# One reciprocal for two steps, a later normalisation, and a new order of SP's transfers in a three-layer attention kernel with a nearest-neighbour branch

## What is computed

```
def chunk_attn(q = k = v = ctx):    # 8 heads of 16 channels, chunks of 64 tokens
    project ctx with W_in to queries, keys and values
    scores = q_chunk . k_chunk / 4 + mask
    attn   = softmax(scores)        # over the 64 keys of the chunk
    return (attn . v_chunk) W_out + b_out
x = layernorm(chunk_attn(ctx) + x)     # layer 0
x = layernorm(chunk_attn(ctx) + x)     # layer 1
idx = top_k(-distance(ctx[0:3] of all token pairs), 30)     # layer 2, the neighbours
feat = spherical coordinates of ctx[0:3][idx] - ctx[0:3]
att = softmax(three small batch-normalised layers of feat)
x = x + sum over the 30 neighbours of att * x[idx]
x = layernorm(chunk_attn(ctx) + x)     # layer 3
```

## Time and profile before

| | us |
|---|---|
| median of 3 executions | 6674.75 (6666.72 to 6677.72) |
| profiled execution | 6667.89 |
| span of the core in it | 6665.9 |
| busy: PE | 5685.7 (85%) |
| busy: DVE | 5886.1 (88%) |
| busy: ACT | 4461.5 (67%) |
| busy: POOL | 3249.3 (49%) |
| mean granted TensorE clock | 0.904 |

### The profile page before, as it was taken

How to read it: one execution, slowest core, us unless ns; L and a number is a source line. 1 busy time by engine, 2 the same in 40 slices (tenths; PEclk the granted TensorE clock), 3 DMA queues, 4 the chain that set the end, 5 groups by cost and what they waited for, 6 DMA issues and landing times. The chain is left out here.

```text
span 6665.9 us, 228315 instructions
## 1 busy us (share of the span) xinstructions
PE 5685.7 (85%) x83284; PEld 3456.0 (52%) x83284; DVE 5886.1 (88%) x8332; ACT 4461.5 (67%) x17049; POOL 3249.3 (49%) x3279
## 2 busy tenths in 40 slices
PE   7888888888888888888888888888839949999998
PEld 3454545455555545545554555555423337677776
DVE  7999999999999999999999999999946588777776
ACT  7787878787787878787877878788822533333333
POOL 3455655555555555555655555555550023333332
PEclk9999988898888999898898998998859979999999
DMA  2333333233333333333233333333241013333332
GB/s 48 89 97 85 93 91 91 84 91 87 100 92 91 97 85 94 91 90 91 85 92 102 91 91 92 93 91 90 80 118 35 0 38 90 90 83 89 87 84 78
DMA packets 633780, 564.50 MB, mean 85 GB/s; under 512 B 535517, under 2 KB 557277, under 8 KB 598653
## 3 DMA queue, kind: packets, MB, share of 16 engines
q1 hardware_dynamic: 632572, 548.75, 29.1%
HBM read 380.55 MB, written 67.24 MB: 67 GB/s over the span
## 5 line engine op out<-in xcount | busy, mean ns | idle before, releaser
L703 ACT ACTIVATE prob<-SC,row_max 128x64 f32<-128x64 f32 x6144 | 1835.3, 327 | 671.7 <-DVE row_max L1032 664.8
L817 POOL TENSOR_TENSOR prob<-prob,row_rec 128x512 f32<-128x512 f32 x768 | 829.9, 1081 | 1897.7 <-DVE row_rec L1040 1897.1
L703 ACT ACTIVATION_READ_ACCUMULATOR prob<-SC,row_max 128x1 f32 x6144 | 1349.0, 220 | 0.0
L1024 DVE FIND_INDEX8 nbr<-top,dist 128x8 uint16<-128x1024 f32 x1024 | 1235.8, 1220 | 0.0
L1017 DVE MAX8 top<-dist 128x8 f32<-128x1024 f32 x1024 | 1194.1, 1207 | 12.6 <-DVE y_b L1055 10.3
L610 PE MATMUL PT<-ident,prob 128*128 128x128 f32 x3072 | 516.1, 295 | 573.9 <-ACT prob_t L710 563.2
L610 PEld LDWEIGHTS PT<-ident,prob 128*128 128x128 f32 x3072 | 383.6, 151 | 1076.8 <-issue 1033.2
L589 PE MATMUL SC<-k_bd,q_t 128*64 128x256 f32 x6144 | 935.8, 430 | 0.0
L1019 DVE MATCH_REPLACE8 dist<-top,dist 128x1024 f32<-128x1024 f32 x768 | 925.2, 1210 | 0.0
L1816 DVE TENSOR_TENSOR d_oh_a<-lo,iota_a 128x4096 bf16<-128x4096 bf16 x256 | 584.4, 2293 | 255.2 <-PE DM L1667 254.8
L1708 ACT ACTIVATE dense<-DM 128x512 f32<-128x512 f32 x512 | 305.6, 597 | 746.3 <-PE DM L1667 746.1
(11 more groups left out here) (194 smaller groups left out, 9538.6 us busy)
## 6 DMA issues: line engine op xcount, KB each, us to landing
low_all<-low_scratch SPq DMA_DIRECT2D x256, 1024.0 KB, 4.9
k_bd<-k_t SPq DMA_DIRECT2D x3072, 16.0 KB, 1.9
placed<-compact SPq DMA_DIRECT2D x256, 192.0 KB, 3.7
ctx<-in_ctx SPq DMA_DIRECT2D x32, 512.0 KB, 4.0
mask<-in_mask SPq DMA_DIRECT2D x32, 512.0 KB, 7.8
xb<-in_x SPq DMA_DIRECT2D x32, 512.0 KB, 4.3
x_scratch<-xb SPq DMA_DIRECT2D x32, 512.0 KB, 4.7
y_scratch<-y_b SPq DMA_DIRECT2D x32, 512.0 KB, 6.6
```

The lines of the kernel that those rows point to most:

```text
L703: last = act.activation(prob[:, s % 4, g * CHUNK:(g + 1) * CHUNK], SC[:, s % 2, g * CHUNK:(g + 1) * CHUNK], ACT.Exp, bias=row_max[:, s % 2 ...
L817: pool.tensor_tensor(pr, pr, row_rec[:, r % 2, :].unsqueeze(2).to_broadcast([128, 8, CHUNK]), ALU.mult).then_inc(normed, 1)
L1024: last = dve.max_index(nbr[:, uu % BPB, t, k * 8:(k + 1) * 8], best, row)
```

## The change

Four edits. The lag of the normalisation goes from one step to two (`LAG_SUM`), and `row_sum` and `row_rec` get four buffers in place of two. DVE takes one reciprocal of 16 columns in every even step, for the two steps before it, in place of one of 8 columns in each step. POOL normalises step s-2 in its step s. On SP, the three pieces on the low index bytes (out, tiles 0 and 1, the later tiles) go to the head of the step, before the keys; and the indices themselves (`nbr`) go out in step 7, after the keys, and not in step 5.

```diff
--- before.py
+++ after.py
@@ -37,7 +37,7 @@
 HALF = T // 2
 
 
-LAG_SUM, LAG_T, LAG_PV, LAG_O, LAG_Y = 1, 3, 4, 5, 6
+LAG_SUM, LAG_T, LAG_PV, LAG_O, LAG_Y = 2, 3, 4, 5, 6
 LAG_BN, LAG_LN, LAG_TOP = 7, 8, 2
 
 
@@ -192,8 +192,8 @@
         prob = sb("prob", [128, 4, 512])
         prob_t = sb("prob_t", [128, 2, 512])
         row_max = sb("row_max", [128, 2, 8])
-        row_sum = sb("row_sum", [128, 2, 8])
-        row_rec = sb("row_rec", [128, 2, 8])
+        row_sum = sb("row_sum", [128, 4, 8])
+        row_rec = sb("row_rec", [128, 4, 8])
         o_t = sb("o_t", [128, 2, HALF])
         y_b = sb("y_b", [128, 2, T])
         stats = sb("stats", [128, 2, 6])
@@ -427,8 +427,31 @@
                 return real(i, v + BPB, BPB)
 
             def step(i, s):
+                v = lagging(i, s, LOW_OUT_AT)
+                if v is not None:
+                    b = i * BPB + v
+                    sp.wait_ge(low_ready, START + b + 1)
+                    alone(sp)
+                    rows = dram["low"][b].rearrange("t (g q k) -> q g t k", q=4, k=KP)
+                    for q in range(4):
+                        sp.dma_start(rows[q], low[32 * q:32 * q + 32, :, :]).then_inc(low_out, 16)
+                v = lagging(i, s, LOW_IN_AT)
+                if v is not None:
+                    sp.wait_ge(low_out, START + (i * BPB + v + 1) * 64)
+                    alone(sp)
+                    for t in range(2):
+                        load_low(i, v, t)
+                at = lagging_tile(i, s, SELECT_AT)
+                if at is not None and at[1] + 2 < NT:
+                    load_low(i, at[0], at[1] + 2)
                 if real(i, s, STEPS) and s % 2 == 0 and real(i, s // 2 + KEY_BUFS - 1, STEPS // 2):
                     keys_of_heads(i, s // 2 + KEY_BUFS - 1)
+                v = lagging(i, s, LOW_IN_AT + 1)
+                if v is not None:
+                    b = i * BPB + v
+                    sp.wait_ge(topped, START + (b + 1) * NT)
+                    alone(sp)
+                    sp.dma_start(dram["nbr"][b], nbr[:, v % BPB, :, :].rearrange("p t k -> p (t k)")).then_inc(nbr_out, 16)
                 ub = s // BSTEPS + 1
                 if real(i, s, STEPS) and real(i, ub, BPB):
                     if s % BSTEPS == COLS_OUT_AT:
@@ -450,23 +473,6 @@
                     landed(sp, x2_out, i, v)
                     alone(sp)
                     sp.dma_start(xb[:, v % BPB, :], dram["x"][i * BPB + v + BPB]).then_inc(x_in[v % BPB], 16)
-                v = lagging(i, s, LOW_OUT_AT)
-                if v is not None:
-                    b = i * BPB + v
-                    sp.wait_ge(topped, START + (b + 1) * NT)
-                    alone(sp)
-                    sp.dma_start(dram["nbr"][b], nbr[:, v % BPB, :, :].rearrange("p t k -> p (t k)")).then_inc(nbr_out, 16)
-                    sp.wait_ge(low_ready, START + b + 1)
-                    alone(sp)
-                    rows = dram["low"][b].rearrange("t (g q k) -> q g t k", q=4, k=KP)
-                    for q in range(4):
-                        sp.dma_start(rows[q], low[32 * q:32 * q + 32, :, :]).then_inc(low_out, 16)
-                v = lagging(i, s, LOW_IN_AT)
-                if v is not None:
-                    sp.wait_ge(low_out, START + (i * BPB + v + 1) * 64)
-                    alone(sp)
-                    for t in range(2):
-                        load_low(i, v, t)
                 v = lagging(i, s, 6)
                 if v is not None:
                     b = i * BPB + v
@@ -475,9 +481,6 @@
                     sp.dma_start(dram["y3"][b], y_b[:, y_half(LAYERS * v + 2), :]).then_inc(y3_out, 16)
                     if more(i, v):
                         sp.dma_start(mask[:, v % BPB, :], dram["mask"][b + BPB].broadcast_to([128, T])).then_inc(mask_in[v % BPB], 16)
-                at = lagging_tile(i, s, SELECT_AT)
-                if at is not None and at[1] + 2 < NT:
-                    load_low(i, at[0], at[1] + 2)
                 v = lagging(i, s, OWN_AT)
                 if v is not None:
                     b = i * BPB + v
@@ -698,10 +701,10 @@
                 if real(i, s, STEPS):
                     act.wait_ge(maxed, START + i * STEPS + s + 1)
                     act.wait_ge(transposed, at_least(i, START + i * STEPS + s - 3, START))
-                    act.wait_ge(recip_ready, at_least(i, START + i * STEPS + s - 1, START))
+                    act.wait_ge(recip_ready, at_least(i, START + i * (STEPS // 2) + s // 2 - 1, START))
                     for g in range(8):
                         last = act.activation(prob[:, s % 4, g * CHUNK:(g + 1) * CHUNK], SC[:, s % 2, g * CHUNK:(g + 1) * CHUNK], ACT.Exp,
-                                              bias=row_max[:, s % 2, g:g + 1], accum_out=row_sum[:, s % 2, g:g + 1])
+                                              bias=row_max[:, s % 2, g:g + 1], accum_out=row_sum[:, s % 4, g:g + 1])
                     last.then_inc(exped, 1)
                 r = s - LAG_T
                 if real(i, r, STEPS):
@@ -812,9 +815,9 @@
                 u = s // BSTEPS
                 r = s - LAG_SUM
                 if real(i, r, STEPS):
-                    pool.wait_ge(recip_ready, START + i * STEPS + r + 1)
+                    pool.wait_ge(recip_ready, START + i * (STEPS // 2) + r // 2 + 1)
                     pr = prob[:, r % 4, :].rearrange("p (h k) -> p h k", h=8)
-                    pool.tensor_tensor(pr, pr, row_rec[:, r % 2, :].unsqueeze(2).to_broadcast([128, 8, CHUNK]), ALU.mult).then_inc(normed, 1)
+                    pool.tensor_tensor(pr, pr, row_rec[:, r % 4, :].unsqueeze(2).to_broadcast([128, 8, CHUNK]), ALU.mult).then_inc(normed, 1)
                 part = s % BSTEPS - SPLIT_AT
                 if real(i, s, STEPS) and 0 <= part <= SPLITS and real(i, u + 1, BPB):
                     split_row(i, u + 1, part, START + i * STEPS + r + 1)
@@ -1034,10 +1037,10 @@
                 if real(i, s, STEPS) and s % BSTEPS == MASK_AT and real(i, u + 1, BPB):
                     mask_rows(i, u + 1)
                 r = s - LAG_SUM
-                if real(i, r, STEPS):
-                    dve.wait_ge(exped, START + i * STEPS + r + 1)
-                    dve.wait_ge(normed, at_least(i, START + i * STEPS + r - 1, START))
-                    dve.reciprocal(row_rec[:, r % 2, :], row_sum[:, r % 2, :]).then_inc(recip_ready, 1)
+                if real(i, r, STEPS) and r % 2 == 0:
+                    dve.wait_ge(exped, START + i * STEPS + r + 2)
+                    dve.wait_ge(normed, at_least(i, START + i * STEPS + r - 2, START))
+                    dve.reciprocal(row_rec[:, r % 4:r % 4 + 2, :], row_sum[:, r % 4:r % 4 + 2, :]).then_inc(recip_ready, 1)
                 r = s - LAG_Y
                 if real(i, r, STEPS) and r % 4 == 3:
                     jj, uu = place(r)
```

## The result

The changed kernel takes 6757.17 us (median of 4 executions, 6746.05 to 6760.6) against 6675.35 us before (4 executions, 6666.72 to 6677.72): a ratio of 1.0122, with an interval of 1.0109 to 1.0136. It is slower, as forecast, but by 82 us and not by 25, and outside my range (6600 to 6750).

What follows compares the result with a forecast made beforehand. The prediction took DVE to be the bound. Its terms, -109.8 (low bytes) + 62 (keys) + 84 (clock) - 11 (reciprocals), gave +25 us: 6693 on the profiled execution, 6700 on the median's scale, range 6600 to 6750.

Steps and rivals of the forecast that it cites:

- What the change takes away: Step 2: tile 6 is issued where the keys were, so DVE's wait for low bytes goes; -109.8 us.
- What the new order adds, the keys: Step 6's keys queue behind tile 1's load; PE idles in step 10, DVE waits in steps 10 and 11; +62 us.
- two patterns: DVE's wait in steps 10 and 11 alternates by batch between 2.8 and 1.3 us; mean 2.05, over 30 batches.
- the late pattern: The batch worked out first: tile 1 goes out behind the late last fetch, and DVE waits 2.8 us in steps 10 and 11.
- The clock: PE's clock falls to 0.50 behind the new idle stretch in step 10; 2.8 us in each of 30 batches, +84 us.
- Rival (1): Scores of step 10: PE's clock does not fall at the new gap, or its loss is absorbed; -59, 6616; chance 0.20.
- Reciprocals: DVE issues 384 fewer, the 384 left are wider; -11 us, bounds -23 and +19.
- The estimate of -41 us: Net for the reciprocals by the skill's fixed cost of a DVE operation, 384 fewer giving 60 us; not adopted.
- Normalisation later: POOL's product a step later is hidden behind other work, and nothing is won; 0 us in the sum.
- Rival (4): Step 13: the late normalisation is exposed too, 2 us in each of 30 batches; +85, 6760; chance 0.10.

Runs made afterwards that it cites:

- filler_16: The changed kernel with 16 products of 128x128 f32 put into PE's step 10, ahead of its wait for the keys; 6699.8 us, ratio 1.0041.
- late_loads_first: The kernel before with only the loads of tiles 2 to 7 moved ahead of the keys of their step; 6560.56 us, ratio 0.983.
- late_norm_only: The changed kernel with SP's order as before; the paired reciprocals and the later normalisation stay; 6604.82 us, ratio 0.9902.
- sp_order_only: The kernel before with all of the new order on SP; reciprocals and normalisation lag as before; 6710.36 us, ratio 1.0066.
- keys_split: The changed kernel with four of step 6's eight keys issued ahead of the loads of tiles 0 and 1, four behind; 6698.03 us, ratio 1.0033.

## Why the prediction was wrong, by its own steps

**What the change takes away: right.** -109.8 us, and the table of after has no such wait.

**What the new order adds, the keys: right in mechanism, 62 us forecast, 78 us measured** (`filler_16`, where the clock is at 1.00). I had two patterns, 2.8 and 1.3 us, and took their mean, with the sentence that the batches "go to and fro" between them. That sentence failed. In batches 4 to 31 of the kernel before, the last fetch ended late (over 13.6 us after the maxima of step 6) in 13 of 28; after, in 26 of 28. The mean went from 13.4 to 14.3 us. It is not the new gap that does this: late_loads_first has neither stall nor gap, and there it is 27 of 28 (mean 14.3). I read it so, without a run that tests this alone: with the stall of step 2 gone, DVE comes to step 6 sooner while PE's fetch doesn't, and the late pattern holds nearly always. 2.8 us in each of 30 batches is 84 us. A pattern that a stall made was carried into a kernel without the stall. PE's idle stretch I had put at 4.7 us; it is 4.4. In part the sum was off: 5.7 us for eight keys puts the start of the last at 2022.8, not 2023.0.

**The clock: right, 84 forecast, 75 measured.** That is 2.5 us a batch against my 2.8. Rival (1) falls with it. The loss is 75 of 6757 us, 1.1%. The Trainium skill (TensorE: Matmul & The Clock Gate, Part 1) puts the ramp at under 1% of a typical kernel's span, but it says so of the warm-up of a kernel's first matmuls. Here the clock fell in 30 batches, so the sentence was no support for rival (1). The loss is small as a share, but nearly as large as the whole net effect of the change.

**Scores elsewhere: not forecast.** 171.3 less 153.5 leaves 17.8 us of new waits outside steps 10 and 11, 12 of them in steps 0 and 1. They come with the late normalisation: late_norm_only has 17.1 us of them, sp_order_only 0.7. By what path is open.

**Reciprocals: right.** The source view of after has them:

```profile
L1043 DVE RECIPROCAL row_rec<-row_sum x384: 229/240/254, 43.8 to 4924.7; 128x16 f32<-128x16 f32 x192
```

240 ns, as forecast. With DVE's waits and the longer `hot` taken out, odd steps became 0.07 us shorter and even ones 0.04 longer, over 384 of each: -11 us, the forecast figure. The price by start-to-start time held. The estimate of -41 us, from the Trainium skill (VectorE: DVE Perf Modes, the part on the TRN2 errata), did not.

**Normalisation later: this step failed, on both sides.** I had written "so nothing is won", since DVE did not wait for exponentials. I had looked at who waits for the normalised values and not at what POOL does in the time that it no longer waits. There is a gain: the coordinates leave 3.2 us sooner, which by itself takes 75 us of low-byte wait away (late_norm_only, 0.9902). In the full change this cannot be seen, for SP's new order removes the same wait already; two cures of one stall don't add up. And there is a loss, which I had not listed in any form: POOL, moved in time, runs into `hot`, 30 us. Beside the new order the pairing leaves only costs and the small gain of the reciprocals: 30 (`hot`) + 23 (scores, 215.0 less 191.6) - 11 = +42 us. The attention stretch is 40.8 us longer than in sp_order_only (4887.3 less 4846.5), and so the full change is worse than its order alone: 6757 against 6710.

**Rival (4)** gave 6760, within 3 us of the result, and is still false. Its mechanism was PE waiting for late products, and the place was right: PE waits 33 times for 81.5 us, against 9.9 before, and 30 of these, 79.3 us, are for the product of POOL's step 13, one in each batch. But DVE has no wait for scores in steps 12 to 16 in this kernel, and late_norm_only has the same wait on PE (91.2 us) and is faster than before. It lies beside other work, as the forecast had it.

**Range and sum.** The upper end, 6751 (+76), was the late pattern in every batch with the full clock loss. Keys and clock together stayed 44 us below that (153 against 197). What carried the time over it are the two costs that come with the late normalisation and stood in no term: the `hot` collision and the scores elsewhere, 48 us. From +25: +16 (keys) -9 (clock) +18 (other scores) +30 (`hot`) = +80.

## What to carry to other kernels

Before transfers are moved up in an in-order queue, list for each step what stands behind each of its waits afterwards; one load that waits, ahead of eight small copies in one step of 24, turned a gain of 1.2% into a loss of 1.2%, and moving only the loads of tiles 2 to 7 gained 1.7%. When a change takes a recurring stall away, don't average over the patterns that the stall made: ask which of them is left. And an engine off the critical path that gets free earlier has two effects to price, what it releases sooner and what it now runs beside.

## What the runs showed of the hardware

**DVE and POOL hold each other up.** The bf16 table of line 1094 takes 1.27 us alone and 2.05 us in the mean of step 2 when a POOL `tensor_tensor` is under way. In the rows above, POOL's product ran to 2015.34 and DVE's had come at 2014.37. The Trainium skill (SBUF — State Buffer, Who interferes with whom) states that a DVE operation in a two-port mode, which a `tensor_scalar` can enter, and a GpSimd operation take a shared pair of ports by an exclusive lock, and that the second blocks until the first is done. By that rule, with the trace's durations, `hot` would take 0.97 + 1.27 = 2.24 us and POOL's next product, blocked from 2015.42 until DVE's end at 2016.43, 1.01 + 1.00 = 2.01. The trace has 2.06 and 1.86, so it agrees within 0.2 us. The first half holds beyond this pair: in the attention stretch of the changed kernel 69 of these tables took over 1.35 us, at the start of each a POOL `tensor_tensor` was running, and each lasted 1.08 us longer than the rest of that product.

**Small copies right behind a large one are late.** Keys of 16 KB land 1.9 us after their issue as a rule. In the kernel before, the first key issued behind a load of 1 MB landed 3.9 us after its issue (median of 91), the fourth 2.6, the fifth 2.3 and the eighth 1.9. With four keys behind the load PE went on 3.7 us after the last issue (keys_split), with eight 2.0 (the changed kernel).

**The granted clock fell with each of the new idle stretches on PE** of 4.4 us, to 0.56 in the stretch shown, and was back at 1.00 by the scores of step 11. With products in the gap it stayed at 1.00, and a 128x128 product in f32 took 0.23 us (5.62 over 24).
